# Graph attention with a feed-forward chain on one core: the gather loop written out, its maximum kept before the slope, and a layer norm laid in six steps

## What is computed

```
xn = layernorm(x)
# graph attention: row = src, col = dst
Wh = xn @ W + b
e  = leaky(f_dst[col] + f_row[row] + a_b)        # slope 0.2 below zero
m  = segment_max(e, row);  ex = exp(e - m[row])
h  = relu(segment_sum(ex * Wh[col], row) / segment_sum(ex, row))
# linear attention over all nodes, then a feed-forward chain
x1 = layernorm(xn + attention(xn) @ Wo + bo)
x2 = layernorm(x1 + relu(x1 @ W1 + b1) @ W2 + b2)
x  = x + h + x2
x  = x + top2_of_6_experts(layernorm(x))
```

## Time and profile before

| what | value |
|---|---|
| median of three runs | 2507.08 us |
| profiled execution, span | 2505.8 us |
| busy: PE, DVE, ACT, POOL | 2000.0, 1914.7, 1479.9, 1212.4 us |
| gather block | from about 754 to 1980 us |
| mean granted PE clock | 0.894 of full speed |

### The profile page before, as it was taken

One profiled execution on the slowest core, in us unless ns is written; L12 is line 12 of the kernel. 1 busy time (PEld: TensorE's weight loads), 2 busy tenths in 40 slices (PEclk: granted clock), 3 DMA queues, 4 the chain that ended last, 5 costly groups with the idle time before them and its releaser, 6 DMA issues. The chain is left out here.

```text
span 2505.8 us, 55059 instructions
## 1 busy us (share of the span) xinstructions
PE 2000.0 (80%) x10267; PEld 1596.8 (64%) x10268; DVE 1914.7 (76%) x6441; ACT 1479.9 (59%) x4950; POOL 1212.4 (48%) x1141
## 2 busy tenths in 40 slices
PE   2888856688855898898888888988989665199997
PEld 1444435577744677677777767767767554188886
DVE  7877689999966898898898898898899763045553
ACT  3566457233304787778788778777878662033332
POOL 0000000011127777777777777777771067455554
PEclk9899967799967899999999989989999866599998
DMA  4200000011113444444444434344440355345553
GB/s 138 54 25 28 25 5 21 13 54 25 21 24 104 119 113 118 114 111 117 113 113 118 110 105 113 111 115 114 117 113 29 92 145 141 86 76 93 94 97 57
DMA packets 125788, 211.73 MB, mean 84 GB/s; under 512 B 35583, under 2 KB 78492, under 8 KB 125476
## 3 DMA queue, kind: packets, MB, share of 16 engines
q0 software_dynamic: 71952, 141.08, 23.7%
q1 hardware_dynamic: 48866, 60.24, 8.2%
q10 hardware_dynamic: 4658, 7.46, 1.0%
HBM read 152.62 MB, written 49.70 MB: 81 GB/s over the span
## 5 line engine op out<-in xcount | busy, mean ns | idle before, releaser
L1283 POOL DMA_INDIRECT area<-wh_table,area x860 | 866.5, 1008 | 284.6 <-issue 257.0
L1586 PE MATMUL bank<-area 128*126 x2008 | 532.7, 412 | 29.4 <-ACT area L1513 20.5
L1586 PEld LDWEIGHTS bank<-area 128*126 128x126 f32 x2008 | 386.2, 203 | 105.0 <-issue 49.5
L1322 DVE TENSOR_SCALAR area<-iota_row,area 128x126 f32<-128x126 f32 x1004 | 343.4, 357 | 0.4 <-issue 0.2
L1499 ACT ACTIVATE area<-iota_row,area 128x126 f32<-128x126 f32 x753 | 269.9, 390 | 0.0
L2077 POOL DMA_INDIRECT out_dram<-area x108 | 169.5, 1569 | 159.3 <-DVE area L2136 142.6
L1513 ACT ACTIVATE area<-area 128x126 f32<-128x126 f32 x753 | 242.4, 385 | 0.0
L515 POOL IOTA acc_mem<- 50x860 f32 x1 | 0.8, 846 | 457.5 <-DVE area L784 457.5
L1606 PE MATMUL bank<-area 128*128 128x250 f32 x800 | 211.4, 410 | 0.0
L1617 PE MATMUL bank<-area 128*125 128x256 f32 x800 | 197.1, 389 | 0.0
L1332 DVE TENSOR_REDUCE area<-bank 125x1 f32<-125x512 f32 x251 | 171.0, 681 | 26.6 <-issue 13.6
(11 more groups left out here) (387 smaller groups left out, 4468.4 us busy)
## 6 DMA issues: line engine op xcount, KB each, us to landing
area<-moe_rows SPq DMA_DIRECT2D x54, 264.0 KB, 2.8
area<-wh_table,area POOLq DMA_INDIRECT x860
area<-area SPq DMA_DIRECT2D x19, 387.0 KB
wh_table<-area SPq DMA_DIRECT2D x50, 126.0 KB
xn<-in_x_dram SPq DMA_DIRECT2D x25, 250.0 KB
x_rows<-area SPq DMA_DIRECT2D x25, 250.0 KB
area<-x_rows ACTq DMA_DIRECT2D x24, 250.0 KB
area<-in_L_ffn_expert_w_dram SPq DMA_DIRECT2D x3, 1536.0 KB, 12.2
```

The costliest lines, as they stand in the source:

```text
L1283: g.indirect_dma_start(out=gath[:, (i + GT) % RS, :], out_offset=None, in_=table, in_offset=bass.IndirectOffsetOnAxis(ap=idx_tab[:, i:i + ...
L1322: ins = V.tensor_scalar(xm[:, b, t, :], iota_row[:, :], rowl[:, j % 10, t:t + 1], fdc[:, b, t:t + 1], ALU.is_equal, ALU.mult)
L1586: last = T.matmul(bank[US][0:RW, 0:WROW], sm[:, b, t, :], gath[:, bass.ds(place + t, 1), :].rearrange("p a w -> p (a w)"), start=(t == 0), ...
```

## The change

The hardware loop becomes straight code. The running maximum is kept before the slope (`peak`), so that five short DVE instructions for each group become two. The maximum of the column terms is no longer found from the data; a bound from the squared weights is used, and the table row holds the term with that bound added in a further column, so that the addition `shifted` goes away and `mark` reads its scalar straight from the gathered rows. The old maximum needed for rescaling is read from the stored row word; the parts are stored as 32-bit words whose upper halves are read as bf16. The layer norm of a feed-forward chunk, which stood in slots 0 and 2 on DVE with its root in slot 1, goes into slots 0 to 5 with the root in slot 3. Outside the loop, the setup loses a chain of short DVE instructions and gains a few at the start; two register instructions are added to a register load on SP and on DVE in the third block.

```diff
+TW = D + 3
...
-    with eng.Fori(1, NC // 2) as it:
+    for it in range(1, NC // 2):
...
-                step(V.tensor_reduce(scol, bank[KV][:, 0:R], AX.X, ALU.min))
...
-                step(V.tensor_scalar(scol, scol, cdst, None, ALU.add))
-                step(V.tensor_scalar(shift[:, :], scol, -1.0, 1.0, ALU.mult, ALU.add))
-                step(V.tensor_scalar(fr[:, :], frd[:, :, 1], csrc[0:R, :], None, ALU.add))
-                step(V.tensor_copy(own_all[:, :, 0], fr[:, :]))
-                step(V.tensor_tensor(fr_c[:, :], fr[:, :], own_all[:, :, 0], ALU.subtract))
-                step(V.tensor_copy(own_all[:, :, 1], fr_c[:, :]))
-                step(V.tensor_tensor(own_all[:, :, 2], fr_c[:, :], own_all[:, :, 1], ALU.subtract))
-                V.tensor_scalar(fr_c[:, :], fr[:, :], shift[0:R, :], None, ALU.subtract).then_inc(shift_done, 1)
+                step(V.tensor_scalar(own_all[:, :, 0], frd, csrc[0:R, :], None, ALU.add))
+                step(V.tensor_tensor(own_all[:, :, 1], own_all[:, :, 0], own_bits[:, :, 0], ALU.subtract))
+                V.tensor_tensor(own_all[:, :, 2], own_all[:, :, 1], own_bits[:, :, 1], ALU.subtract)
+                V.tensor_scalar(fr_c[:, :], own_all[:, :, 0], shift[0:R, :], None, ALU.subtract)
...
+                    dve.wait_ge(sq_sum, 1)
+                    step(V.tensor_scalar(shift[:, :], bank[2][:, 0:1], 8.0, 9.0, ALU.mult, ALU.add))
+                    step(V.tensor_tensor(bias_g[:, D:D + 1], bias_g[:, D:D + 1], shift[:, :], ALU.add))
...
-                    V.tensor_scalar(fdc[:, b, :], dst_terms(j), shift[:, :], None, ALU.add).then_inc(d_x, 1)
...
+                    V.scalar_tensor_tensor(peak[0:R, bass.ds(r, 1)], gmax[0:R, b:b + 1], fr_c[:, bass.ds(r, 1)], peak[0:R, bass.ds(r, 1)],
+                                           ALU.add, ALU.max).then_inc(d_m, 1)
...
+                    V.scalar_tensor_tensor(new[0:R, b:b + 1], peak[0:R, bass.ds(r, 1)], 0.2, peak[0:R, bass.ds(r, 1)],
+                                           ALU.mult, ALU.max).then_inc(d_m, 1)
...
+                parts = {0: [feed_sum], 1: [feed_bias], 2: [feed_moments, feed_totals], 3: [feed_centre], 4: [feed_scale], 5: [feed_out]}
...
-                together(dve, [(2, group_peak), (-1, load_place), (4, score_sum), (2, row_score), (0, shifted), (4, score_edge),
-                               (2, row_leaky), (0, mark(0)), (4, score_leaky), (2, new_max), (0, mark(1)), (4, score_less_max),
-                               (0, mark(2)), (2, old_less_new), (0, mark(3)), (2, keep_max), (4, own_weight), (5, gather_up)], feed)
+                together(dve, [(2, group_peak), (-1, load_place), (4, score_sum), (0, mark(0)), (2, row_peak), (4, score_edge),
+                               (0, mark(1)), (2, row_leaky), (4, score_leaky), (0, mark(2)), (4, score_less_max),
+                               (0, mark(3)), (4, own_weight), (5, gather_up)], feed)
...
-                    if slot == 1 and (not isinstance(c[0], int) or at(c) > 0):
+                    if slot == 3 and (not isinstance(c[0], int) or at(c) > 0):
...
-                together(act, roots, [(3, own_high), (3, apart([0])), (3, own_mid), (2, spread), (3, own_low), (4, edge_exp), (3, apart([1, 2])), (3, rescale),
-                                       (4, weigh), (-1, own_rows)], feed)
+                together(act, roots, [(3, rescale), (3, apart([0])), (3, own_first), (2, spread), (3, own_second), (4, edge_exp), (3, apart([1])), (3, own_third),
+                                       (3, apart([2])), (4, weigh), (-1, own_rows)], feed)
```

More of the change, by code:

```diff
@@ L51 @@
 LAG = 5
-SPARE = 820
+SPARE = 940
 SLOT, TAB_SLOTS = 6, 8
@@ L245, in gps_kernel @@
         more = take(128)
[L246 to L247 removed]
+        rstd_all, nmr = (take(NT)[0:R] for _ in range(2))
+        mvs, frd = take(NT, 2)[0:R], take(NT)[0:R]
         ti = wbase.rearrange("p k b -> p (k b)").bitcast(I32)
@@ L318, in gps_kernel @@
         int50 = smallt[6].bitcast(I32)
-        gcol, scol, neg1, cdst, csrc, tcol, wcol, tq0, tq1 = (take(1) for _ in range(9))
+        gcol, csrc, tcol, wcol, tq0, tq1 = (take(1) for _ in range(6))
         srci, dsti = wpos.bitcast(I32), bpos.bitcast(I32)
@@ L1042, in _ @@
                 pe.wait_ge(w_ready, 1)
+                for k in range(2):
+                    last = T.matmul(bank[2][:, 0:1], ones[:, :], wsq[:, k:k + 1], start=(k == 0), stop=(k == 1))
+                last.then_inc(sq_sum, 1)
+                pe.wait_ge(w_ready, 2)
                 def transposes(t):
```

204 lines of the change are left out of this document (104 added, 100 removed).

## The result

The changed kernel takes 2484.1 us (median of four runs, 2483.21 to 2487.28), the kernel before beside it 2509.6 us (2505.85 to 2512.56). The ratio is 0.9912, 95% interval 0.9897 to 0.9926: 0.9% faster, and 5 us above the forecast of 2479. By the two medians the gain is 25.5 us, by the ratio 22. So few executions don't fix it more closely: the median of the kernel before lies between 2506.9 and 2509.1 us beside the experiments of the usual speed. The profiled execution took 2484.0 us with a span of 2482.2, against a forecast span of 2477.8.

What follows compares the result with a forecast made beforehand. Steps and POOL's gathers ran nearly level, with POOL a floor up to group 239. 1883.6 + 46.6 + 22.0 = 1952.2 us for the block's end, 28.0 off, gave span 2477.8 and time 2479 us, range 2467 to 2493.

Steps and rivals of the forecast that it cites:

- What bounds it: Gather block: step pipeline at 47.8 us a chunk against POOL's gathers at 46.8, which set a floor up to group 239.
- The loop written out: Gather loop: straight code gives 3.0 us a chunk, 44.8 against 47.8, below POOL's 46.8; instruction streaming costs nothing.
- rival one: Only the written-out loop counts; last chunk stays at 44.8 us, tail at 25.5; 2486 us; 14 in 100.
- Start of the block: Setup before the gathers: shorter DVE chain gains 1.4 us, bounds 0.4 to 1.8.
- Group 239: First group needing the last tiles: starts at 1883.6 us against 1905.75, 22.2 gained, with a backlog of 1.5.
- The last chunk: Ten steps behind the loop: 42.5 us against 44.8, bounds 40 and 44.8; group 239 to 250 gains 2.4.
- ACT: Steps: the maximum's last part moved behind the exponential costs nothing, as PE is already the longer chain at 4.10 us.
- The tail: Last six steps of the gather block: 22.0 us against 25.5, 3.5 gained, bounds 0 and 5.
- The third block: Behind the gather block: moves with the barrier, stays at 525.6 us; added register operations cost nothing.
- Two: Rival: POOL's gathers go faster, every 1.298 us instead of 1.311; 2468 us; 8 in 100.
- Three: Rival: exposed address preparations and a fetch waiting on ACT cost 0.6 us a step; about 2507 us; 6 in 100.
- Four: Rival: PE at half clock in the POOL-paced steps, 8.2 instead of 4.1 us; about 2571 us; 6 in 100.

Runs made afterwards that it cites:

- e6: Kernel before, with its loop, its 860 indexed transfers replaced by 215 plain ones of the same bytes; ratio 0.855 on the slow chip, span 2486.8 us.
- e8: Changed kernel with the bounds test dropped from the indexed transfers, on a chip of usual speed; 2440.6 us, ratio 0.9726.
- e5: Changed kernel with its 860 indexed transfers replaced by 215 plain ones of the same bytes; ratio 0.8174 on the slow chip, span 2377.6 us.
- e3: Changed kernel with the layer norm packed into slots 0 and 2 again and its root in slot 1; 2509.9 us, ratio 1.0014.
- e1: Kernel before with only its hardware loop written out, plus register operations that keep a count positive; 2487.6 us, ratio 0.9918.
- e2: Changed kernel with the hardware loop put back; 2487.3 us, ratio 0.9912.
- e4: Changed kernel with five short DVE instructions added to the setup chain of the row terms; 2485.6 us, ratio 0.9913.
- e10: e3 with the third part of the maximum put ahead of the exponential on ACT; 2492.2 us, ratio 0.9931.
- e9: Kernel before with the loop written out and the norm in slots 0 to 5, root in slot 3, nothing else; 2483.6 us, ratio 0.9904.
- e7: Changed kernel with the bounds test dropped from the indexed transfers, on the slow chip; 2845.2 us, ratio 0.9778.

## Why the prediction was right, point by point

**What bounds it.** Two nearly level chains, the steps at 47.8 and POOL at 46.8 us a chunk (47.1 measured in the changed kernel's middle): shown. e6 has the steps at 47.6 with POOL free. e8 moves the end by POOL's pace alone, e5 shows the steps at 43.1 without POOL, and e3 shows the kernel back at 2510 once the steps need 47.8 again.

**The loop written out.** Forecast 2486 for it alone (rival one), measured 2487.6 in e1, and costing the long instruction stream at nothing was right. The row I read it from was the wrong one: "the largest of these gaps is 2.8 us" names the norm's wait. The turn has a gap of the same size, half as often. And 44.8 was no fair price for a straight chunk. The last chunk's slot 1 runs from group 249 in the row below to the 1964.59 of the earlier trace rows, 3.06 us, because its step 251 has no new group to mark; in the loop slot 1 of a chunk without a turn takes 3.95 us, and the whole chunk 46.0.

```profile
1961.53 0.66 DVE L1332 TENSOR_REDUCE area<-bank 125x1 f32<-125x512 f32 x1
```

So the loop written out was worth 1.9 us a chunk and not 3.0, and the steps were to be 0.8 us under POOL's 46.8, not 2.0. In e1 the 46.9 us a chunk are POOL's pace, so the steps alone were not seen there. The forecast held because 46.0 is still under POOL; that much of it is luck. Nor is the loop the only way there: e2 keeps it and is as fast.

**Start of the block.** The step failed in size: 753.0 forecast, 748.0 measured, and 5.3 us gained on average where I took 1.4, and had 1.8 as upper bound. I priced the removed instructions by their length on DVE. What came with the new setup besides is a higher clock of PE in the stretch behind them, 0.81 to 0.85 instead of 0.70 to 0.77. I had costed the clock at nothing for the whole kernel without looking at the setup. The shorter chain doesn't account for it, as e4 shows, and what does stays open.

**Group 239.** 1883.6 forecast, 1884.4 measured, but from two errors that cancel: the gathers began 5.0 us earlier, and went at (1878.2 - 748.0) / 859 = 1.316 us instead of 1.311, which is 4.1 us. The last gather was 0.9 us early. 1.311 was the stretch up to 1390 us of one execution; in the other traces with the test on the indices the whole lies between 1.314 and 1.317 as long as POOL leads. The backlog was 3.2 us instead of 1.5: 6.2 from the last gather's start, less the 3.0 of the earlier trace rows. It is inside the bounds, and varies with the kernel (1.3 in e1, 5.2 in e8 and 6.6 in e10, by the same working).

**The last chunk.** 42.5 forecast, 42.5 measured (own rows), and shown by e1 (45.2) and e9 (42.6) to come from the norm's spread alone. The exact match is partly luck. e2, e4, e5 and e7 have the changed kernel's steps word for word in this chunk and take 43.5 to 44.1: their slot 2 is 5.6 to 6.0 us long at a clock of 0.69 to 0.72, where the changed kernel and e8 have 4.6 us at 1.00. So the 0.8 us that I added for a rest of the half clock didn't occur in the profiled execution, and other slots were 0.6 us dearer than my 41.7; in four others it occurred and was more. Two rows of the windows of slot 2 show it, first the changed kernel, then e4:

```profile
1897.20:1901.79 4.59, 3.51 (x20) 2.63 (x20) 4.17 (x19) 4.59 (x18) 0.00 (x0) 1.00 0.01 4
```

```profile
1899.58:1905.62 6.04, 5.70 (x24) 4.52 (x24) 4.19 (x18) 4.71 (x18) 0.00 (x0) 0.72 0.01 3
```

The make-up was less right too. I had 4.05, 4.05, 4.5, 4.3 and 4.3 for slots 0 to 4; measured are 4.7, 3.35, 4.6, 4.65 and 4.7, with 3.9 in slot 5. The 0.25 us off DVE's ordinary step are real (between 872 and 1828 us, some 200 steps, DVE's busy time is 744.4 us instead of 848.6, which is 0.5 a step) but in slots 6 to 9 PE holds the step at 4.10, and in the others they are not what ends the wait. e9 without them is as fast.

**ACT.** "I cost it at nothing: PE is already the longer chain" was right in the sum and wrong as a reason. e3 and e10 show that the new place of the third part costs 1.4 us in the last chunk, and 15 to 18 us in the end, if the norm stays in two slots. What covers it is the spread norm, and not PE's length. The two edits stand or fall together, and my terms treated them as independent.

**The tail.** This is the term that missed most of the sum: 22.0 forecast, 24.2 measured, inside the bounds of 0 to 5 gained. PE's clock is 0.51 for 10 of these 24 us, so at 1.2 GHz: eight products of `total` (L1601) take 3.80 us there, and 1.91 at the tail's start. I had moved instructions and left out that the PE is half as fast there. The tail before has a low stretch too (0.87 on average, 0.79 after the change); what the forecast lacked is that it could grow. e9, whose tail stays at 1.00, takes 22.9 us. The single tails vary: 22.7 to 24.7 us with the norm spread, 25.5 to 29.0 without.

**The third block** took 526.6 us instead of 525.6, and 525.3 to 528.8 in the other traces. That is scatter.

**The sum.** Block end 1952.2 forecast, 1955.6 measured: +0.8 at group 239, +0.3 to group 250, +2.2 in the tail, with rounding. With the third block's 1.0 this is the span's 4.4 us.

**The rivals.** One gave 2486, and the measured 2484.1 lies nearer to it (1.9 us) than to my 2479 (5.1 us). By the time alone it would be the better forecast. What decides against it is the trace, where it said a last chunk of 44.8 us and a tail of 25.5, and 42.5 and 24.2 were measured, and e9. e1 is this rival as a kernel, and the change lies 3.5 us below it, which is not clear of the scatter. Two, POOL faster by itself, did not happen. Three did not come, though its mechanism, a fetch that waits for ACT, is what the norm in two slots brings about in e3, with the result it names: no difference from before. Four, the half clock, did not come: from 872 to 1828 us the granted clock rose from 0.94 to 0.96. At the time where it was 0.50 it is 0.93, but other steps stand there now. The Trainium skill, in "TensorE: Matmul & The Clock Gate", section "A second HAM failure mode: psum-queue depth-cycling", describes a kernel in which frequent short idling between groups of matmuls made the clock swing and cost throughput. The loop here does not agree with it as a whole: by it the granted clock should have fallen, and it rose.

## What to carry to other kernels

When two chains are nearly level, measure each alone before pricing an edit: take the transfers' cost away for one and see what the steps need, and shorten the transfer for the other. Here either half of the change gave about 20 us against the same floor, and both together 22 to 25, while a shorter gather, which the change didn't touch, gave another 44. An instruction that is moved later is free only as long as what covers it stays; try the move with the cover gone. When you take a price from another stretch of the same code, check that its steps do the same work: the last chunk looked like a straight chunk of the loop and was 1.2 us shorter. And one trace that hits a forecast to 0.1 us is one trace; traces of the same ten steps scattered by 1.6 us there.

## What the runs showed of the hardware

The bounds test of an indexed transfer costs 0.052 us of POOL for 128 rows (0.998 against 0.946 us by the median).

On one chip both kernels with indexed transfers that ran there were much slower: the kernel before took 2909 us, and e7 2845, against e8's 2441 for the same program elsewhere. e7's gathers there last 0.95 us like e8's, but POOL stands for ring places. Its timeline, with idle times in brackets:

```profile
1402.72 0.95 POOL L1283 DMA_INDIRECT area<-wh_table,area  x1 [0.30 <-issue]
1413.16 0.95 POOL L1283 DMA_INDIRECT area<-wh_table,area  x1 [9.49 <-SPq L1268]
```

From 872 to 2180 us POOL waits 399.0 us for places in 155 pauses of up to 9.9 us. In 100 us of this stretch (1390 to 1490) the queues move 81 GB/s, and 120 in e8. Plain transfers of the same bytes (e5, e6) showed nothing of it on the same chip. What makes the indexed ones pause there was not tried and stays open.

Executions with the same setup start the gathers up to 6 us apart (743.2 to 749.5), so a single trace doesn't settle a difference of 2 us there.
